# Reciprocals of softmax row sums moved from VectorE to GpSimd in an attention and feed-forward block

## The reference

```python
h = _layernorm(x, axis=-1) * (1 + ca) + sa
q = (h @ Wq + bq).reshape(b, 16, 32, t)          # same for k and v
attn = jnp.einsum('bhdt,bhds->bhts', k, v) * temperature
attn = jax.nn.softmax(attn, axis=-1)
out = jnp.einsum('bhdt,bhts->bhds', q, attn)
x = x + ga * out.reshape(b, t, 512)
```

## Time and profile before

| | |
|---|---|
| median of 3 runs | 2391.11 us (2388.33 to 2392.05) |
| the profiled execution | 2388.49 us |
| its span, first to last instruction | 2386.8 us |
| mean granted clock of TensorE | 0.989 |
| TensorE busy (matmuls) | 2276.0 us, 95% of the span |
| VectorE busy | 1890.3 us, 79% |
| ScalarE busy | 1482.0 us, 62% |
| GpSimd busy | 1370.7 us, 57% |

### The profile page before, as it was taken

The page is one execution under the profiler, slowest core; times in us unless marked ns, Lnnn a source line. Parts: engine busy times, 40 slices in busy tenths (PEclk is TensorE's granted clock), DMA queues, the critical chain, the costliest instruction groups (busy, mean ns, idle before and its releaser), DMA issues.

```text
span 2386.8 us, 41303 instructions
## 1 busy us (share of the span) xinstructions
PE 2276.0 (95%) x12772; PEld 879.3 (37%) x12772; DVE 1890.3 (79%) x2808; ACT 1482.0 (62%) x2616; POOL 1370.7 (57%) x1205
## 2 busy tenths in 40 slices
PE   7999999999999999999999999887989999999996
PEld 2333333333333333333333333221434444444442
DVE  5899999999999999999999999997833553554432
ACT  1788888888888888888888887777311111111110
POOL 4666776667666766667666776553443543544431
PEclk9999999999999999999999999998989999999998
DMA  6332333233343334233333333323412021111100
GB/s 216 71 91 71 85 88 88 69 92 74 81 100 72 79 78 104 63 81 90 77 86 89 75 74 87 73 61 118 116 46 65 23 67 46 41 49 45 58 23 18
DMA packets 123771, 180.83 MB, mean 76 GB/s; under 512 B 44112, under 2 KB 44112, under 8 KB 123480
## 3 DMA queue, kind: packets, MB, share of 16 engines
q1 hardware_dynamic: 113760, 152.30, 26.0%
q0 software_dynamic: 9728, 25.23, 3.5%
HBM read 67.17 MB, written 43.16 MB: 46 GB/s over the span
## 4 chain that ended last, share of the span: by engine, by line
PE 53%; DVE 23%; issue 12%; POOL 5%; ACT 4%; DMA 2%; SPq 1%; DVEq 0%; ACTq 0%; POOLq 0%
DVE nmax L984 16%; PE sc L750 13%; PE sc L737 12%; PE sc L561 9%; PE acc L608 9%; PE pj L583 5%; PE pj L571 3%; POOL x L1326 3%; ACT probs L813 2%; DVE stats L1027 1%; DVE qn L1045 1%; DVE x L1022 1%; ACT room L786 1%; DMA room<-in_L_ffn_W 1%; DVE rinv L1040 1%
## 5 line engine op out<-in xcount | busy, mean ns | idle before, releaser
L813 ACT ACTIVATE probs<-sc,nmax 128x1024 f32<-128x1024 f32 x1024 | 1136.7, 1116 | 241.4 <-DVE nmax L984 236.6
L984 DVE TENSOR_REDUCE nmax<-sc 128x1 f32<-128x1024 f32 x1024 | 1217.9, 1215 | 56.6 <-PE sc L561 50.7
L608 PE MATMUL acc<-probs,qn 128*32 128x512 f32 x4136 | 552.5, 607 | 9.4 <-DVE x L1022 6.9
L886 ACT ACTIVATE probs<-sc,b_col 128x512 f32<-128x512 f32 x128 | 87.9, 687 | 560.4 <-PE sc L737 560.4
L571 PE MATMUL pj<-room 128*128 128x512 f16 x1536 | 394.1, 380 | 0.4 <-ACT qT L803 0.4
L750 PE MATMUL sc<-room,probs 128*128 128x512 f16 x1536 | 352.3, 379 | 8.6 <-DVE probs L1177 8.6
L561 PE MATMUL sc<-stacks 128*128 128x512 f16 x1024 | 309.3, 384 | 20.0 <-ACT probs L813 18.8
L561 PE MATMUL sc<-room 128*128 128x512 f16 x1024 | 308.3, 383 | 18.4 <-issue 7.7
L1175 DVE CAST probs<-probs 128x512 f16<-128x512 f32 x128 | 64.4, 503 | 329.7 <-ACT probs L886 329.5
L750 PEld LDWEIGHTS sc<-room,probs 128*128 128x128 f16 x1536 | 149.5, 98 | 190.7 <-issue 7.1
L571 PEld LDWEIGHTS pj<-room 128*128 128x128 f16 x1536 | 147.8, 98 | 188.7 <-ACT room L786 11.4
(11 more groups left out here) (147 smaller groups left out, 2334.8 us busy)
## 6 DMA issues: line engine op xcount, KB each, us to landing
room<-room SPq DMA_DIRECT2D x512, 64.0 KB, 2.0
stacks<-room SPq DMA_DIRECT2D x512, 64.0 KB, 2.0
h_rows<-hbuf SPq DMA_DIRECT2D x132, 128.0 KB, 2.3
out<-base SPq DMA_DIRECT2D x132, 128.0 KB, 2.5
room<-in_L_attn_x SPq DMA_DIRECT2D x96, 128.0 KB, 2.7
rows<-mod_rows SPq DMA_DIRECT2D x32, 256.0 KB, 4.1
room<-in_L_ffn_W SPq DMA_DIRECT2D x8, 1024.0 KB, 5.2
probs<-in_L_wmod SPq DMA_DIRECT2D x4, 1024.0 KB, 8.0
```

The lines of the kernel that those rows point to most:

```text
L608: mm = nc.tensor.matmul(acc[at:at + DH, :], qn[:, (p // 2) % 2, p % 2, h2, :], probs[:, (2 * p + h2) % PROBS, half * D:(half + 1) * D], st ...
L813: nc.scalar.activation(probs[:, u % PROBS, :], slot(g, ring_at(p, h2)), ACT.Exp, bias=nmax[:, u % PROBS:u % PROBS + 1], accum_out=rsum[:, ...
L886: nc.scalar.activation(g32[:, f % 2, :], ff[f % 2], ACT.Gelu_apprx_tanh, bias=b1_col[:, f:f + 1], scale=1.0 / WS).then_inc(gelu_done, 1)
L984: nc.vector.tensor_reduce(nmax[:, u % PROBS:u % PROBS + 1], slot(g, ring_at(p, h2)), AX.X, ALU.max, negate=True).then_inc(max_done, 1)
```

## The change

The reciprocals leave VectorE's list. GpSimd computes them as `rsum` to the power of minus one, with the same wait for the exponentials, ahead of the wait for `qn` that precedes each portion, and so behind the portion before. `q_over_sums` on VectorE keeps its wait for `inv_done`, which GpSimd now raises. A constant `minus_one` is set once, and one more `over_sums` stands behind the last group.

```diff
+        minus_one = sb("minus_one", [P, 4], F32)
...
+            nc.vector.memset(minus_one[:], -1.0)
...
             def q_over_sums(b, g, quad):
                 par, p = quad % 2, 2 * quad
                 s, i = p // NQ, p % NQ
-                dve.wait_ge(slot_free, freed(b, g, ring_at(p + 1, 1)) + SLOTS)
-                nc.vector.reciprocal(rinv[:, par, :], rsum[:, par, :]).then_inc(inv_done, 1)
                 if quad == 0:
                     dve.wait_ge(q_evac, b * (2 * GB) + 2 * (g + 1))
                 dve.wait_ge(inv_done, b * (GB * PAIRS // 2) + g * (PAIRS // 2) + quad + 2)
...
+            def over_sums(b, g, quad):
+                par, p = quad % 2, 2 * quad
+                pool.wait_ge(slot_free, freed(b, g, ring_at(p + 1, 1)) + SLOTS)
+                nc.gpsimd.tensor_tensor(rinv[:, par, :], rsum[:, par, :], minus_one[:], ALU.pow).then_inc(inv_done, 1)
+
             def behind_qn(b, g, j):
+                over_sums(b, g - (j == 0), (j - 1) % (PAIRS // 2))
                 wait_alone(qn_done, b * (GB * PAIRS // 2) + g * (PAIRS // 2) + j + 2)
...
             body(LAST, True)
+            over_sums(B, -1, PAIRS // 2 - 1)
             residual(B, 0)
```

## The result

The changed kernel takes 2542.84 us (median of 4 runs, 2541.21 to 2545.24) against 2391.04 us before (2388.33 to 2392.05): a ratio of 1.0635, 95% interval 1.062 to 1.0651. The forecast was 2547, within 2490 to 2633. The profiled execution took 2543.33 us with a span of 2541.6, which is 154.8 us more than before.

A forecast was written before the change was run, and what follows sets the result against it. TensorE was taken to bound the kernel, busy in 48.43 of 48.54 us per group. 2388.5 us plus 146 (5.2 per group, 28 groups) plus 12 (last batch) gave 2547, range 2490 to 2633.

The forecast's parts named there:

- x = 1.0: Length in us of one 128x4 power on GpSimd, taken between 0.71 and 1.42.
- The rival of a cheap power: Power takes 0.33 us, twice VectorE's reciprocal; kernel slower but by half as much, 2450 to 2460 us; chance 0.05.
- The four rings: Quads 3 to 6: `qn`, next portion, its power and next `qn` wait in turn; 5.6 us longer per group.
- The other quads: Quads 7, 0, 1, 2: VectorE's savings give -0.4 us per group, between -0.8 and +0.6.
- the prediction's condition: In quads 7, 0, 1, 2 VectorE's saving counts only as far as PE gained a lead during the stalls.
- The covers: VectorE's next row maxima, 1.14 us in quad 1 and 1.37 in quad 7, just hide the power at x = 1.0.
- Batches 0 to 6: 28 groups, each 5.2 us longer, 146 us in all.
- Batch 7: Last batch, four groups: ring longer by less, 3 us per group, 12 in all, from 0 to 24.
- The set-up: One more memset in the set-up was said to cost nothing that can be read.
- That the reciprocal is ready in time: Rival: all eight powers come before DVE needs them; 2341 us at best, 2388 at worst; faster by over 0.2%: chance 0.03.
- the 82 us that were worked out: VectorE time freed: 43.0 us of reciprocals plus 39 us from `qn` no longer colliding with GpSimd.
- The clock: PE's granted clock stays at 1.00 despite some 10% idle; a dear power or a clock fall together had chance 0.06.

The follow-up runs named there:

- the run without reciprocals: The kernel before with VectorE's reciprocals removed; VectorE waits for the exponentials as before and multiplies by a constant tile: 2379.15 us, ratio 0.9958.
- the run with four quads: The changed kernel with GpSimd computing reciprocals only in quads 7, 0, 1, 2, VectorE those of 3 to 6, and a later store wait: 2383.42 us, ratio 0.9965.
- the run inside the portions: The changed kernel with the powers of quads 3 to 6 in the middle of GpSimd's portions, and a later store wait: 2490.94 us, ratio 1.0413.
- the run of unread powers: The kernel before plus GpSimd powers of a constant at the change's places, into a tile nobody reads; VectorE keeps its reciprocals: 2458.06 us, ratio 1.0293.

## Why the prediction was right

*What bounds.* Right: PE's 99% meant that DVE's relief is worth little by itself; 10 to 12 us of 43 by the run without reciprocals, and in batches 0 to 6 only 4.4 of 37.

*The power's length.* x = 1.0 was taken between 0.71 and 1.42; it is 1.018. The bounds came from a row, the place between them was a choice, so that it is right within 2% is luck. The rival of a cheap power, x = 0.33, fell with this row: the power takes six times the 167 ns of the reciprocal.

*The four rings.* They were to last 7.92, 7.22, 7.77 and 7.28 us and sum to 30.19; the medians over batches 0 to 6 are 7.89, 7.39, 7.66 and 7.44, sum 30.38. One step was left out in quads 4 and 6: POOL waits 0.16 us for the end of its own product before the power, a wait that the program before has too. In quad 5 the ring is 0.1 shorter because `qn` 4 takes 0.29 and not 0.38. In the group shown quad 4 took 7.70, above its median, with the hand-over of 0.54. DVE's waits in front of these four `qn` are 7.5 us per group by the medians, more than the 5 to 6 that were expected, since DVE comes to them sooner.

*The other quads.* Right in sign, too small in size: -0.4 was taken, with -0.8 as the end, and they went from 23.96 to 22.85 us (sums of medians), -1.1. Most of it is quad 7, 6.55 to 5.86. Before, DVE waited there for PE's scores in every one of the 28 groups, 0.31 us at the median:

```profile
949.45 1.23 DVE L984 TENSOR_REDUCE nmax<-sc 128x1 f32<-128x1024 f32 x1 [0.31 <-PE sc L561]
```

In the changed kernel it does so in 3 groups: the stalls in quads 3 to 6 have given PE a lead. `qn` 6, which opens the quad, is also 0.32 us shorter. Without reciprocals and without stalls the quad stays at 6.55, so the lead is what counts there. Quads 0 and 2 give 0.2 us each also in that run, without any lead of PE; there the prediction's condition was wrong. The covers held as worked out: DVE waits 0.11 us in quad 1 and 0.20 in quad 7.

*Batches 0 to 6.* 5.2 us per group were taken, 4.8 measured (53.69 against 48.90), 134 us in place of 146.

*Batch 7.* 12 us were taken from a bare estimate of 3 per group; it is 17.2. The reason that was given, that the ring is longer by less there, was not tested.

*The set-up.* Put at nothing, which was wrong. The first `qn` starts at 75.2 us in place of 70.4. POOL's first power stands behind a wait for a store that its list had ahead of the first portion; before, that wait had 10 us of POOL's idle time for itself, and now DVE's first `qn` is behind it. The rows of POOL and DVE:

```profile
74.09 1.02 POOL L1365 TENSOR_TENSOR rinv<-rsum,minus_one 128x4 f32<-128x4 f32 x1 [9.52 <-DMA mod_rows<-base]
```

```profile
75.15 0.29 DVE L1045 TENSOR_TENSOR qn<-qT,rinv 128x128 f32<-128x128 f32 x1 [2.68 <-POOL rinv L1365]
```

So 2.7 of the 4.8 us are a wait for the power; the other 2 lie ahead of it, as in the run without reciprocals. The question for each moved step, which waits stand ahead of it in its new list, was put for the loop and not for the first turn.

*The sum.* 134 + 17.2 + 4.8 - 1.2 (the feed-forward stage) = 154.8, the difference of the spans. That the forecast is only 4 us off is in part luck: batches 0 to 6 came out 12 us below it, since the other quads gave back more, and the set-up and batch 7 10 us above.

*The rivals.* That the reciprocal is ready in time held only in quads 7, 0, 1 and 2, which the run with four quads uses. The collisions of `qn` did vanish (113.3 to 74.0 us), and with the reciprocals that is the 82 us that were worked out. They do not show in the kernel's time: DVE comes to `qn` sooner and waits longer there. By the profiled spans DVE is busy 72.0 us less (the router's products take 6 us more) and idle 226.8 us more: together the 154.8 us. Of its idle time 9.1 us stood in front of `qn` before, and 237.9 stand there now.

*The clock.* Wrong in a small thing: "I expect no fall to the lower level". See below.

## What to carry to other kernels

Before a step is moved to an engine with idle time, follow it once round: what does the new engine do ahead of it in its list, whom does that work wait for, and does this close a ring with the reader of the step? The length of each ring, portion and hand-overs and operation, is read from the trace and compared with the time between two readers; an average load of 68% says nothing about it. A late engine also has a price without any wait, where its operations hold up those of another engine that has little time to spare. Here the move paid only in the quads where the other engine was idle.

## What the runs showed of the hardware that was not expected

POOL's power costs 0.708 us on two columns and 1.018 on four; a straight line through these two points, an estimate, has 0.155 us for each column and some 0.4 that do not depend on them. A product on four columns costs 0.201.

A `qn` of 0.29 us takes up to 2.44 us when a POOL operation of two inputs on long rows began 0.07 us ahead of it, and ends 0.15 us behind it. One of a single input does the same: in the run inside the portions `qn` 6 takes 1.13 us beside the split of 1.05 us that began 0.06 us ahead of it. A power, which also reads two inputs, does not: there 31 `qn` began 0.22 to 0.24 us into a power of 0.72 us and took 0.28. From that run:

```profile
978.84 0.72 POOL L1284 TENSOR_TENSOR rstd<-var,minus_half 128x2 f32<-128x2 f32 x1
979.06 0.28 DVE L1045 TENSOR_TENSOR qn<-qT,rinv 128x128 f32<-128x128 f32 x1
...
1000.04 1.05 POOL L1293 TENSOR_SCALAR room<-room 128x1024 f16<-128x1024 f32 x1
1000.10 1.13 DVE L1045 TENSOR_TENSOR qn<-qT,rinv 128x128 f32<-128x128 f32 x1 [0.32 <-POOL rinv L1366]
```

The Trainium skill ("SBUF — State Buffer", section "Who interferes with whom") says that the access which VectorE and GpSimd share is an exclusive lock, and that the order of issue decides who is held up. The traces agree for the long operations, with 1.12, 1.13, 2.28 and 2.44 us against 0.29, and differ for the powers, beside which `qn` takes 0.28. So what costs time in the run of unread powers is not the powers themselves but the later place of the long operations behind them. How much this is worth in total (`qn` and the router's product 61 and 31.5 us more with unread powers, 84 and 60.5 inside the portions) had not been foreseen when the unread powers were planned.

PE's granted clock fell to 1.2 GHz for a short time in 13 of the 28 groups of batches 0 to 6, where it was at 2.4 GHz throughout before. A stretch of the changed kernel, columns as in the earlier trace rows, and PE's timeline around it:

```profile
856.00:859.00 3.00, 3.00 (x12) 0.49 (x11) 1.22 (x1) 2.89 (x8) 2.89 (x2) 0.50 0.44 100
```

```profile
855.51 0.96 PE L562 MATMUL sc<-room 128*128 128x512 f16 x2 [1.95 <-ACT probs L814]
856.40 1.94 PE L609 MATMUL acc<-probs,qn 128*32 128x512 f32 x8
...
860.47 1.06 PE L609 MATMUL acc<-probs,qn 128*32 128x512 f32 x8
```

PE stood idle for 1.95 us up to 855.51, behind the stalled row maxima; then the clock was low and the eight matmuls of `products` took 1.94 us in place of 1.06. All 13 falls came behind such an idle time of about 2 us; 21 idle times of PE of over 1.5 us in these batches had no fall behind them. The groups with a fall are 0.35 us longer on average than those without (53.88 against 53.53), and 0.06 at the median. If all of it were the clock's, that would be some 5 us of 152; that it is was not shown.
